# Sixteen-head attentions: parts stored after head 0's copies, head 1's maxima laid beside head 0's scores, units of maxima announced singly

## Chip, cores and metric

One NeuronCore of a Trainium2 chip runs the whole program. The metric is the device time in microseconds (us) of one execution. Three runs of the kernel before took 5205.0, 5204.46 and 5199.28 us; the median is 5204.46 us.

## The reference, cut to what matters

The program is a four-layer hybrid network on 2,048 tokens of width 128. Each step is `x = x + block(layernorm(x))`. Three of its blocks are softmax attentions with 16 heads of width 8, and the change touches these:

```python
# L0_attn_b: rotary, causal.  L2_attn_b and L3_attn_b: every query sees every key.
q, k, v = (x @ Wq + bq), (x @ Wk + bk), (x @ Wv + bv)      # 2048 x 128, 16 heads of 8
s = q_h @ k_h.T / sqrt(8)                                  # per head, 2048 x 2048
p = softmax(s)                                             # L0: keys after the query masked
out = concat_h(p @ v_h) @ Wo + bo
```

A fourth attention (L3_attn_a, local windows) shares the helper that prepares heads, in a variant that is not doubled (below).

## The kernel before, in words

**Splitting and rows.** `prepare_heads` (line 732) splits q and k, each 128 rows (16 heads of 8) by 2,048 tokens in float32, into three bfloat16 parts whose sum is nearly exact (DVE lines 768 to 777, ACT lines 785 to 791), makes two doubled copies of q's lesser parts (line 781) and evicts V (line 794). SP meanwhile copies head 0's 8 rows of each part, SBUF to SBUF, into `qs[0]` and `ks[0]` (`copy_queries`, `copy_keys`, lines 714 to 722: 12 transfers of 32 KB, counted on `rows_in[0]`). ACT then issues the stores of all parts to DRAM (`store_part`, `store_twice`, lines 724 to 729: 8 transfers of 512 KB, counted on `stored`). The block ends when every engine has come to its end, and only then does the next one begin.

**The head loop.** `head_loop` (line 843) is one block in which five engines run their own hand-written orders:

- *Maxima.* PE multiplies 48 rows of bfloat16 parts into scores for a block of 128 queries against up to 1,024 keys (`max_pass`, line 982, matmuls on line 994) and DVE takes the row maximum (line 1133). Such a piece is a unit; there are U = 32 per head without a mask and U = 24 with it. Two PSUM tiles `mps` alternate, so unit x needs unit x - 2 to be taken (line 990). Causal units that cross the diagonal get a mask by another matmul (line 1000). In the causal loop the units of heads 1 and up are issued in pairs, the matmuls of both, then the masks, and one announcement, `mx_ready` plus 2, at the end (line 1001). The first 8 pairs of a head hold an unmasked unit of 1,024 keys and then a masked one of 128 to 512; in the last 4 pairs both are masked.
- *Turn.* After a head's last unit DVE joins its maxima (`join_max`, line 1115), POOL splits them in three (line 427), PE turns them (`turn_max`, line 1003, matmul on line 1008), ACT copies them to `mT` (line 1086), and a DMA puts them into three rows of `qs` (line 1096 on ACT's queue for head 0, line 946 on SP's for the others). DVE joins head h only after unit 0 of head h + 1 (line 1134).
- *Scores.* For each step n of S (S = 64 without a mask, 40 with it) PE computes a tile of 128 keys by up to 512 queries with 123 rows (line 1018), the maximum already subtracted by those three rows, and ACT takes the exponential (line 1105). Three PSUM tiles `sps` alternate. `product` (line 1024) multiplies a group of such tiles by V, 4 or 6 steps late.
- *Copy-out.* After the last product of head h - 1, ACT copies the sums (`copy_out`, line 1088, instruction on line 1092) behind its exponential of step n = OUT = 6 of head h (line 1109). The first product of head h waits for that (line 1028).

**Interleaving.** `due(h, n)` (line 906) says how many units must have been issued by step n of head h. Before the scores begin PE has issued U + 8 units: all of head 0, 3 of head 1, then the turn of head 0, then 5 more of head 1 (lines 1046 to 1053). From then on due rises by U per head, in twos. The turn of head h + 1 stands behind step TURN = S - 7 of head h.

**SP's order.** It waits for all stores (line 957), loads head 1's rows (12 transfers, `load_rows`), then the upper half of head 0's rows (6 transfers on `m_in[0]`), `load_products` of heads 0 and 1 (4 transfers each), a table, then head 2's rows, and from then on one head ahead. `scores` of head h waits on `m_in` (line 1014), `max_pass` of a head's unit 0 on `rows_in` (line 988).

## Time and profile before

| | |
|---|---|
| median of 3 runs | 5204.46 us |
| profiled execution | 5199.7 us (its span in the trace: 5197.9 us) |
| mean granted TensorE clock | 0.918 of 2.4 GHz |
| PE busy | 4488.1 us, 86% of the span, 22,389 matmuls |
| DVE busy | 3223.0 us, 62% |
| ACT busy | 2648.4 us, 51% |
| POOL busy | 976.2 us, 19% |

The causal attention (tiles named 9_heads, 5_head_rows, 8_prepare) lies between 343 and 920 us of the span, the other two (39_heads, 36_head_rows, 38_prepare; and 64_heads, 59_head_rows, 63_prepare) between 2442 and 3185 and between 4164 and 4906 us. In a timeline row stand the start in us, the duration in us of the instructions merged into it, the engine, the line, the operation, output and inputs, the number of instructions, and in brackets how long the engine had been idle and what released it. PEq, ACTq and SPq are the sequencers; a DMA row there is the time in which the transfer was issued, not that in which it moved. A releaser "PEq L755" is the end of the `prepare_heads` block. PEclk is the granted clock: 0.50 is 1.2 GHz, 1.00 is 2.4 GHz.

### The profile page before, as it was taken

The page shows a single profiled execution, that of the slowest core. Times are in us where ns is not written, and L with a number is a line of the kernel's source. Part 1 is how long each engine was busy: PE and PEld are TensorE (multiplying, and loading weights), DVE is VectorE, ACT ScalarE, POOL GpSimd, SP SyncE. Part 2 cuts the span into 40 slices and gives each one's busy share as a digit, 9 for nine tenths or more (in the row PEclk, how much of TensorE's full clock was granted, in tenths as well). Part 3 has the DMA queues.
Part 4 walks back from the last instruction along what each step waited for, and adds up shares of the span by engine and source line. Part 5 has one row for each costly group of instructions (what it writes and reads, how often), then busy time and mean ns, then how long its engine had stood idle before and what let it go on. Part 6 is the DMA issues. An engine that isn't in the chain of part 4 may idle for free. (4 is left out here: it accounts for less than half of the span.)

```text
span 5197.9 us, 65865 instructions
## 1 busy us (share of the span) xinstructions
PE 4488.1 (86%) x22389; PEld 1663.4 (32%) x22441; DVE 3223.0 (62%) x4634; ACT 2648.4 (51%) x4913; POOL 976.2 (19%) x920
## 2 busy tenths in 40 slices
PE   6978888795189999867999997688869889999899
PEld 3432222442033333243122223355544412222244
DVE  4366664435865555254988883437963488888433
ACT  2325666334224444433588885344433348888633
POOL 0000000000038777800000000047940000000000
PEclk8979999897599999978899998898979979999999
DMA  1011110000000000001100000110000010000000
GB/s 62 20 67 35 35 35 20 17 16 0 7 1 3 5 3 5 5 28 37 36 28 28 27 18 2 56 62 3 1 9 16 11 68 26 26 26 26 3 21 20
DMA packets 44620, 118.99 MB, mean 23 GB/s; under 512 B 14463, under 2 KB 15863, under 8 KB 43287
## 3 DMA queue, kind: packets, MB, share of 16 engines
q1 hardware_dynamic: 37235, 98.19, 5.7%
q10 hardware_dynamic: 4524, 15.78, 0.8%
q8 instruction: 166, 2.72, 0.2%
q0 software_dynamic: 2560, 1.19, 0.1%
q14 instruction: 135, 1.11, 0.1%
HBM read 87.89 MB, written 19.01 MB: 21 GB/s over the span
## 5 line engine op out<-in xcount | busy, mean ns | idle before, releaser
L1133 DVE TENSOR_REDUCE 64_heads_mx<-64_heads_mps 128x1 f32<-128x1024 f32 x512 | 604.1, 1220 | 64.3 <-PE 64_heads_mps L994 63.1
L1133 DVE TENSOR_REDUCE 39_heads_mx<-39_heads_mps 128x1 f32<-128x1024 f32 x512 | 604.1, 1220 | 64.3 <-PE 39_heads_mps L994 63.2
L1105 ACT ACTIVATE 64_heads_p<-64_heads_sps 128x512 f32<-128x512 f32 x1024 | 552.8, 596 | 111.2 <-PE 64_heads_sps L1018 107.3
L1105 ACT ACTIVATE 39_heads_p<-39_heads_sps 128x512 f32<-128x512 f32 x1024 | 552.7, 596 | 111.3 <-PE 39_heads_sps L1018 107.3
L2106 ACT ACTIVATE 27_latent_heads_p<-27_latent_heads_ring 128x512 f32<-128x512 f32 x512 | 277.3, 595 | 385.4 <-PE 27_latent_heads_ring L2025 374.1
L1133 DVE TENSOR_REDUCE 9_heads_mx<-9_heads_mps 128x1 f32<-128x1024 f32 (+7 forms) x384 | 334.2, 908 | 179.7 <-PE 9_heads_mps L1000 173.3
L2124 DVE TENSOR_REDUCE 27_latent_heads_mx<-27_latent_heads_ring 128x1 f32<-128x512 f32 x512 | 323.1, 684 | 197.4 <-PE 27_latent_heads_ring L2005 197.4
L1105 ACT ACTIVATE 9_heads_p<-9_heads_sps 128x512 f32<-128x512 f32 (+3 forms) x640 | 304.3, 535 | 190.0 <-PE 9_heads_sps L1021 161.6
L1018 PE MATMUL 64_heads_sps<-59_head_rows_qs,59_head_rows_ks 123*128 123x512 bf16 x1024 | 311.3, 386 | 4.9 <-ACT 64_heads_p L1105 4.9
L1018 PE MATMUL 39_heads_sps<-36_head_rows_qs,36_head_rows_ks 123*128 123x512 bf16 x1024 | 310.9, 385 | 5.2 <-ACT 39_heads_p L1105 5.2
L1981 POOL TENSOR_TENSOR 27_latent_heads_psum<-27_latent_heads_psum,27_latent_heads_p 128x1024 f32<-128x1024 f32 x112 | 263.1, 2349 | 87.8 <-ACT 27_latent_heads_p L2106 87.8
L2021 PE MATMUL 27_latent_heads_ring<-27_latent_heads_qc,23_mla_mem_keys 64*128 64x512 f32 x1024 | 272.7, 609 | 3.4 <-DMA 24_mla_loop_mem_mrow<-27_latent_heads_mT 3.4
L1042 PE MATMUL 39_heads_ops<-39_heads_p,L2b_v 128*9 128x512 f32 x2048 | 267.8, 595 | 0.2 <-ACT 39_heads_osb L1092 0.2
L1042 PE MATMUL 64_heads_ops<-64_heads_p,L3b_v 128*9 128x512 f32 x2048 | 267.8, 595 | 0.2 <-ACT 64_heads_osb L1092 0.2
L1976 POOL TENSOR_TENSOR 27_latent_heads_psum<-27_latent_heads_psum,27_latent_heads_p 128x1024 f32<-128x1024 f32 x112 | 263.3, 2351 | 23.0 <-ACT 27_latent_heads_p L2106 23.0
L2005 PE MATMUL 27_latent_heads_ring<-23_mla_mem_keys,27_latent_heads_qc 64*128 64x512 f32 x1024 | 265.1, 609 | 1.9 <-DVE 27_latent_heads_mx L2124 0.5
L994 PE MATMUL 64_heads_mps<-59_head_rows_ks,59_head_rows_qs 48*128 48x512 bf16 x1024 | 187.6, 403 | 23.3 <-PEq L755 15.3
L994 PE MATMUL 39_heads_mps<-36_head_rows_ks,36_head_rows_qs 48*128 48x512 bf16 x1024 | 187.7, 403 | 18.1 <-PEq L755 10.0
L1018 PE MATMUL 9_heads_sps<-5_head_rows_qs,5_head_rows_ks 123*128 123x512 bf16 (+3 forms) x640 | 183.4, 353 | 11.5 <-ACT 9_heads_p L1105 4.3
L427 POOL CAST 64_heads_mparts<-64_heads_m 128x16 bf16<-128x16 f32 x16 | 3.1, 196 | 973.9 <-DVE 64_heads_m L1119 973.9
L615 DVE TENSOR_TENSOR 4_experts_hg<-4_experts_hr,4_experts_gps 128x512 f32<-128x512 f32 x128 | 88.0, 687 | 147.8 <-ACT 4_experts_hr L602 147.5
L615 DVE TENSOR_TENSOR 67_experts_hg<-67_experts_hr,67_experts_gps 128x512 f32<-128x512 f32 x128 | 88.0, 688 | 146.4 <-ACT 67_experts_hr L602 146.1
(1119 smaller groups left out, 7456.7 us busy)
## 6 DMA issues: line engine op xcount, KB each, us to landing
44_hale_masks_qs<-scratch_q_parts SPq DMA_DIRECT2D x45, 96.0 KB
44_hale_masks_ks<-scratch_k_parts SPq DMA_DIRECT2D x45, 96.0 KB
4_experts_wbuf<-in_L0f_experts SPq DMA_DIRECT2D x8, 514.0 KB, 3.5
12_experts_wbuf<-in_L0f_experts SPq DMA_DIRECT2D x8, 514.0 KB, 3.4
58_experts_wbuf<-in_L3f_experts SPq DMA_DIRECT2D x8, 514.0 KB, 3.5
67_experts_wbuf<-in_L3f_experts SPq DMA_DIRECT2D x8, 514.0 KB, 3.5
5_head_rows_qs<-scratch_q_parts SPq DMA_DIRECT2D x47, 64.0 KB
5_head_rows_ks<-scratch_k_parts SPq DMA_DIRECT2D x47, 64.0 KB
```

What stands on the lines that cost most here:

```text
L615: dve.tensor_tensor(hg[n % SLOTS][:], hr[n % SLOTS][:], gps[n // NF % 2][:], ALU.mult).then_inc(hg_ready, 1)
L994: ins = pe.matmul(mps[x % 2][:, b:b + n], qs[h % SETS][low:low + SIX, tile(i)], ks[h % SETS][low:low + SIX, 1024 * half + b:1024 * half + ...
L1018: ins = pe.matmul(sps[e % SB][:, 0:CW - off], ks[h % SETS][0:SUM_ROWS, tile(j)], qs[h % SETS][0:SUM_ROWS, c * CW + off:(c + 1) * CW], star ...
L1042: ins = pe.matmul(ops[row:row + ROW, off:CW], Vt[:, j, h, :], p, start=(s == 0), stop=(causal or s == NG - 1), tile_position=(0, row), ski ...
L1105: act.activation(pslot[x % PS][:, 0:CW - off], sps[e % SB][:, 0:CW - off], ACT.Exp, scale=SCALE / 2).then_inc(ex_done, 1)
L1133: dve.tensor_reduce(mx[h % 2][:, i, half:half + 1], mps[x % 2][:, 0:w], AX.X, ALU.max).then_inc(mx_taken, 1)
L1976: pool.tensor_tensor(psum[:, 0, :], so_far, slot(p, h)[:], ALU.add).then_inc(added_even, 1)
L1981: pool.tensor_tensor(psum[:, 1, :], so_far, slot(p, h)[:], ALU.add).then_inc(added_odd, 1)
L2005: pe.matmul(bank(number, x)[:], qc[h % 2][half, tile(i)], keys[half, chunk(2 * (u % 2) + x)], start=True, stop=True).then_inc(mx_ready, 1)
L2021: pe.matmul(bank(number, x)[:], keys[half, tile(j)], qc[h % 2][half, chunk(2 * (p % 2) + x)], start=True, stop=False)
L2106: act.activation(slot(p, h)[:, x * CW:(x + 1) * CW], bank(score_number(p, h), x)[:], ACT.Exp, scale=MLA_SCALE).then_inc(ex_done, 1)
L2124: dve.tensor_reduce(mx[:, w // NC, w % NC:w % NC + 1], bank(max_number(w // 2, h), w % 2)[:], AX.X, ALU.max).then_inc(mx_taken, 1)
```

## The change

1. `store_part` and `store_twice` become one `store`. With `doubled` (the three 16-head attentions) ACT no longer calls it in `prepare_heads` but at the start of `head_loop`, after a wait for `rows_in[0]` to reach 12 transfers. Without `doubled` ACT issues the same stores at the same place, behind all its waits instead of part by part.
2. New constants FIRST and WAIT: (0, 8) causal, (4, 0) otherwise. Before the scores PE issues U + FIRST units in place of U + 8, with the turn of head 0 after U + FIRST / 2. In head 0 `due` rises from U + FIRST along a steeper line, from step WAIT on, until it meets the old one; for heads 1 and up it is as before.
3. OUT is 4 instead of 6 in the causal loop.
4. SP loads head 1's rows behind head 0's upper rows and products.
5. Each unit announces itself: an unmasked one behind its own matmuls, a masked one behind its mask.
6. DVE joins head 0's maxima ahead of unit 0 of head 1; for later heads the join stays behind unit 0.

```diff
@@ -721,12 +721,12 @@
             if a == b:
                 eng.dma_start(self.ks[0][DH * i:DH * (i + 1), :], self.k[a][0:DH, :]).then_inc(self.rows_in[0], 16)
 
-    def store_part(self, g, eng, a):
-        eng.dma_start(g.scratch["q_parts"][a], self.q[a][:]).then_inc(self.stored, 16)
-        eng.dma_start(g.scratch["k_parts"][a], self.k[a][:]).then_inc(self.stored, 16)
-
-    def store_twice(self, g, eng, n):
-        eng.dma_start(g.scratch["q_parts"][3 + n], self.twice[n][:]).then_inc(self.stored, 16)
+    def store(self, g, eng):
+        for a in range(3):
+            eng.dma_start(g.scratch["q_parts"][a], self.q[a][:]).then_inc(self.stored, 16)
+            eng.dma_start(g.scratch["k_parts"][a], self.k[a][:]).then_inc(self.stored, 16)
+        for a, t in enumerate(self.twice):
+            eng.dma_start(g.scratch["q_parts"][3 + a], t[:]).then_inc(self.stored, 16)
 
 
 def prepare_heads(g, qT, kT, Vt, Wv, bv, weights, rows):
@@ -793,13 +793,11 @@
                 for c in range(NC):
                     act.activation(Vt[:, c * TPC:(c + 1) * TPC, :, 0:DH], vps[c][:].rearrange("p (t h d) -> p t h d", t=TPC, d=DH),
                                    ACT.Identity).then_inc(v_done, 1)
-                for a in range(3):
+                if not doubled:
                     for s in "qk":
-                        wait_for_part(act, s, a)
-                    rows.store_part(g, act, a)
-                for n in range(len(twice)):
-                    act.wait_ge(two_done, n + 1)
-                    rows.store_twice(g, act, n)
+                        for a in range(3):
+                            wait_for_part(act, s, a)
+                    rows.store(g, act)
 
             @block.sync
             def _(sp):
@@ -853,10 +851,11 @@
     U = len(units)
     SB, PS = 3, 12
     AHEAD = 8
+    FIRST, WAIT = (0, 8) if causal else (4, 0)
     TURN = S - 7
     LATE = 4 if causal else 6
     BURST = 2
-    OUT = 6
+    OUT = 4 if causal else 6
     A = P // HEADS
     N = HEADS * S
     qs, ks, rows_in = rows.qs, rows.ks, rows.rows_in
@@ -903,13 +902,19 @@
         def turned(h):
             return 0 if h == 0 else 2 + (h - 1) * (S + 1) + TURN
 
+
+
         def due(h, n):
-            return min(HEADS * U, U + AHEAD + h * U + (n + 1) * U // (S * BURST) * BURST)
+            steady = min(HEADS * U, U + AHEAD + h * U + (n + 1) * U // (S * BURST) * BURST)
+            if h:
+                return steady
+            begun = max(0, n + 1 - WAIT)
+            return min(steady, U + FIRST + begun * (U - FIRST) // ((TURN - 5 - WAIT) * BURST) * BURST)
 
         def group_of(n):
             return next(j for j, gr in enumerate(groups) if gr[0][0] <= n <= gr[-1][0])
 
-        assert U + AHEAD + (TURN - 4) * U // S >= 2 * U
+        assert due(0, TURN) >= 2 * U
 
         with nc.Block() as block:
             @block.gpsimd
@@ -955,11 +960,11 @@
 
                 sp.wait_ge(rows.filled, rows.FILLED)
                 sp.wait_ge(rows.stored, rows.STORED)
-                load_rows(sp, 1)
                 for a in range(3):
                     load_queries(g, sp, 0, a, qs[0], m_in[0], (1,))
                     load_keys(g, sp, 0, a, ks[0], m_in[0], (1,))
                 load_products(sp, 0)
+                load_rows(sp, 1)
                 load_products(sp, 1)
                 sp.dma_start(spread[:], g.big["head_spread"].rearrange("p (a q) -> p a q", q=P)).then_inc(spread_in, 16)
                 for h in range(HEADS):
@@ -994,11 +999,12 @@
                             ins = pe.matmul(mps[x % 2][:, b:b + n], qs[h % SETS][low:low + SIX, tile(i)],
                                             ks[h % SETS][low:low + SIX, 1024 * half + b:1024 * half + b + n],
                                             start=True, stop=not (diag and b + n == w))
+                        if not diag:
+                            ins.then_inc(mx_ready, 1)
                     for x in xs:
                         _i, _half, w, diag = units[x % U]
                         if diag:
-                            ins = pe.matmul(mps[x % 2][:, w - P:w], g.ident_bf[:], g.mask_q[:], start=False, stop=True)
-                    ins.then_inc(mx_ready, len(xs))
+                            pe.matmul(mps[x % 2][:, w - P:w], g.ident_bf[:], g.mask_q[:], start=False, stop=True).then_inc(mx_ready, 1)
 
                 def turn_max(h):
                     e = turned(h)
@@ -1044,11 +1050,11 @@
                     ins.then_inc(pv_done, 1)
 
                 x = 0
-                while x < U + 3:
+                while x < U + FIRST // 2:
                     max_pass([x])
                     x += 1
                 turn_max(0)
-                while x < U + AHEAD:
+                while x < U + FIRST:
                     max_pass([x])
                     x += 1
                 late = []
@@ -1091,6 +1097,9 @@
                         act.wait_ge(o_out[h % 2], STORED * (h // 2))
                     act.activation(osb[h % 2][:], ops[:], ACT.Identity).then_inc(o_copied, 1)
 
+
+                act.wait_ge(rows_in[0], SIX_COPIED)
+                rows.store(g, act)
                 copy_max(0)
                 act.wait_ge(ex_done, 1)
                 act.dma_start(qs[0][TWICE:SUM_ROWS, :], mT[0][:]).then_inc(m_in[0], 16)
@@ -1129,9 +1138,11 @@
                     i, half, w, _d = units[u]
                     if u == 0 and h >= 2:
                         dve.wait_ge(m_joined, h - 1)
+                    if u == 0 and h == 1:
+                        join_max(0)
                     dve.wait_ge(mx_ready, x + 1)
                     dve.tensor_reduce(mx[h % 2][:, i, half:half + 1], mps[x % 2][:, 0:w], AX.X, ALU.max).then_inc(mx_taken, 1)
-                    if u == 0 and h:
+                    if u == 0 and h >= 2:
                         join_max(h - 1)
                 join_max(HEADS - 1)
                 for i in range(2):
```

## Rows read from the trace of the kernel before

**Rows 1.** Windows, causal and first unmasked attention: length, busy (count) by engine, PEclk, DMA.
```profile
343.00:920.00 577.00, 487.99 (x3128) 140.16 (x3128) 347.86 (x420) 328.06 (x687) 20.66 (x88) 0.94 0.12 40
2442.00:3185.00 743.00, 711.56 (x4152) 147.90 (x4152) 616.92 (x545) 575.02 (x1071) 16.39 (x80) 0.96 0.09 30
```

**Rows 2.** Waits of PE, 440 to 881 us: who for whom, total us, times, longest.
```profile
PE 9_heads_mps L994 <- DVE 9_heads_mx L1133: 23.4, 41, 0.8
PE 9_heads_ops L1039 <- ACT 9_heads_osb L1092: 11.8, 14, 0.8
PE 9_heads_sps L1008 <- POOL 9_heads_mparts L431: 6.2, 13, 0.5
```

**Rows 3.** Timeline of one copy-out of the causal loop.
```profile
568.95 1.47 ACT L1105 ACTIVATE 9_heads_p<-9_heads_sps 128x384 f32<-128x384 f32 x3 [0.97 <-PE 9_heads_sps L1021]
569.83 0.38 PE L1018 MATMUL 9_heads_sps<-5_head_rows_qs,5_head_rows_ks 123*128 123x512 bf16 x1
570.29 0.62 ACT L1092 ACTIVATE 9_heads_osb<-9_heads_ops 128x512 f32<-128x512 f32 x1
571.06 1.06 PE L1039 MATMUL 9_heads_ops<-9_heads_p,9_heads_Vz 128*25 128x512 f32 x8 [0.84 <-ACT 9_heads_osb L1092]
```

**Rows 4.** Timeline around the turn of head 1, causal loop.
```profile
426.79 0.39 PE L994 MATMUL 9_heads_mps<-5_head_rows_ks,5_head_rows_qs 48*128 48x512 bf16 x2
...
427.82 1.23 DVE L1133 TENSOR_REDUCE 9_heads_mx<-9_heads_mps 128x1 f32<-128x1024 f32 x1 [0.55 <-PE 9_heads_mps L1000]
...
430.63 0.24 PE L1008 MATMUL 9_heads_sps<-ident_bf,9_heads_mparts 128*48 128x128 bf16 x1 [0.48 <-POOL 9_heads_mparts L431]
...
432.59 0.49 PE L994 MATMUL 9_heads_mps<-5_head_rows_ks,5_head_rows_qs 48*128 48x512 bf16 x3
...
433.28 1.56 DVE L1133 TENSOR_REDUCE 9_heads_mx<-9_heads_mps 128x1 f32<-128x1024 f32 x2 [1.67 <-PE 9_heads_mps L1000]
...
434.57 0.61 PE L994 MATMUL 9_heads_mps<-5_head_rows_ks,5_head_rows_qs 48*128 48x512 bf16 x3 [0.77 <-DVE 9_heads_mx L1133]
```

**Rows 5.** Timeline, one pair of units of the unmasked loop in its steady part.
```profile
2515.15 0.60 PE L994 MATMUL 39_heads_mps<-36_head_rows_ks,36_head_rows_qs 48*128 48x512 bf16 x4
2515.58 2.36 DVE L1133 TENSOR_REDUCE 39_heads_mx<-39_heads_mps 128x1 f32<-128x1024 f32 x2 [0.50 <-PE 39_heads_mps L994]
```

**Rows 6.** Timeline, from the preparation into the causal head loop.
```profile
356.19 0.36 ACTq L725 DMA_DIRECT2D scratch_q_parts<-5_head_rows_q  x1
...
357.49 0.62 ACT L794 ACTIVATE L0b_v<-8_prepare_vps 128x512 f32<-128x512 f32 x1
...
361.46 2.39 ACTq L729 DMA_DIRECT2D scratch_q_parts<-5_head_rows_twice  x2
...
364.32 1.12 PE L994 MATMUL 9_heads_mps<-5_head_rows_ks,5_head_rows_qs 48*128 48x512 bf16 x3 [8.31 <-PEq L755]
...
367.81 1.92 SPq L818 DMA_DIRECT2D 5_head_rows_qs<-scratch_q_parts  x2
```

**Rows 7.** Timeline, first unmasked attention: into the loop, head 0's turn, first scores.
```profile
2455.26 0.61 ACT L794 ACTIVATE L2b_v<-38_prepare_vps 128x512 f32<-128x512 f32 x1
...
2461.51 1.86 PE L994 MATMUL 39_heads_mps<-36_head_rows_ks,36_head_rows_qs 48*128 48x512 bf16 x4 [9.97 <-PEq L755]
...
2502.90 0.30 PE L1008 MATMUL 39_heads_sps<-ident_bf,39_heads_mparts 128*48 128x128 bf16 x1 [0.85 <-POOL 39_heads_mparts L431]
...
2507.87 1.90 PE L1018 MATMUL 39_heads_sps<-36_head_rows_qs,36_head_rows_ks 123*128 123x512 bf16 x4
```

**Rows 8.** Timeline, causal attention: head 0's turn and first scores.
```profile
396.38 0.30 PE L1008 MATMUL 9_heads_sps<-ident_bf,9_heads_mparts 128*48 128x128 bf16 x1 [0.86 <-POOL 9_heads_mparts L431]
...
404.07 0.61 PE L1018 MATMUL 9_heads_sps<-5_head_rows_qs,5_head_rows_ks 123*128 123x512 bf16 x1 [4.04 <-DMA 5_head_rows_qs<-9_heads_mT]
```

**Rows 9.** Windows: unmasked head 0's maxima, and causal head 0's first scores.
```profile
2462.00:2502.00 40.00, 34.09 (x70) 4.38 (x68) 39.63 (x38) 0.00 (x0) 0.38 (x2) 0.50 0.28 98
404.00:410.00 6.00, 5.83 (x22) 1.58 (x26) 2.21 (x3) 3.88 (x8) 0.00 (x0) 0.62 0.08 31
```

## Prediction

> **What bounds the kernel now.** I read the windows of the attentions first. In the causal one PE is busy 488.0 of 577 us, in the first unmasked one 711.6 of 743 us [rows 1]. So the unmasked loop is full of PE work, and what its steady part could give is small; the causal one leaves 89 us in which PE stands. I then asked PE's waits in the causal loop's steady part: over 441 us, 23.4 us go to DVE's maxima, 11.8 us to the copy-out and 6.2 us to the split ahead of a turn [rows 2]. These come once or a few times per head; over the 13 to 14 heads of that stretch the 41.4 us are 3.0 us a head. Last I read the starts of the three loops, which each come once.
>
> **Part 1, copy-out at step 4 instead of 6 (causal).** ACT's exponentials of steps 4, 5 and 6 begin at 568.95 and take 1.47 us together, the copy-out begins at 570.29, and PE, free at 569.83 + 0.38 = 570.21, waits until 571.06: 0.84 us [rows 3]. Behind step 4 alone (a third of 1.47, 0.49) the copy-out begins at about 569.4 and ends at 570.0, before PE arrives. The last product of the head before was issued at step 3, so it is there. The exponentials of steps 5 and 6 come 0.62 us later; the next score needs that of step 5, done at 570.5, and comes only behind the 1.06 us of products, so this is covered. PE is the bound, so 0.84 us are saved in each of 15 heads: -12.6 us (from below 0, if ACT hands the delay on, to -12.6).
>
> **Part 2, one announcement per unit (causal).** An unmasked unit is ready 0.43 us after its first matmul starts [rows 5]. Around the turn the pair starts at 426.79, so DVE could start at 427.22 and starts at 427.82; it is free by 427.3, so the reduce, the join and the split come 0.5 us earlier, and PE's wait of 0.48 us at the turn goes [rows 4]. That is 14 turns (2 to 15) by 0.48: -6.7 us. At the second pair after the turn PE waits 0.77 us for the reduce that began at 433.28, 0.69 us behind its matmuls at 432.59; with 0.43 in place of 0.69 the wait shrinks by 0.26 [rows 4]. The waits among doubly masked pairs lose only what lies between two masks, some 0.06. So 0.32 by 14.5 heads: -4.6 us. PE's instructions stay the same in number. Bounds: 0 to -12; I take -11.3. In the unmasked loops each unit announced itself already, and OUT stays: 0.
>
> **Part 3, the stores leave the preparation (all three).** ACT finished its last eviction at 358.11, but went on issuing stores until 363.85, and PE started at 364.32 [rows 6]: 0.47 us from ACT's end to PE's start. Now ACT's end is 358.11 and PE starts at about 358.5, if head 0's copies are there; SP issued the last of them before ACT's evictions began, and without stores beside them I expect them just in time: -5.8 us. In the unmasked attention ACT ends at 2455.87 (no row of V's product delays it there), so ACT's end alone would give 2456.3 for 2461.51 [rows 7]; no row shows when the copies landed, which were issued about 1 us later against ACT's end, and I take 2457.0: -4.5 us each (bounds -5.2 to -3). Bounds in the causal one: -6 to -5. What the stores now delay: issuing began at 356.19 and now begins at about 358.6, so SP's first load moves by the same 2.4 us, from 367.81 to some 370.2 [rows 6]. Head 0's ten transfers come first now and have 25 us until they are needed; head 1's twelve come some 10 us behind them, at about 390, while head 0's maxima end at about 388. With WAIT = 8 they are wanted only from 400 on: 0. ACT has nothing else to do in that time.
>
> **Part 4, the join ahead of head 1's unit 0.** It saves one reduce of 1.2 us less its overlap, [rows 4] has 1.23: -1.1 us in each attention.
>
> **Part 5, from head 0's turn to its first score.** In the causal attention it was 404.07 - 396.38 = 7.69 us, and what ended it was the 12 KB transfer of the turned maxima: PE had been idle for 4.04 us when it landed [rows 8]. SP's loads were under way beside it. They still are: 0. In the unmasked one it was 4.97 us, and PE was filling it with units, not waiting [rows 7]. Now only 2 units stand there, about 2.3 us, and the transfer is issued some 5.6 us earlier while SP's loads end 2 to 3 us later, so it lies in the middle of them as the causal one did: 7.7 us, +2.7 each. Bounds: 4.2 (the shortest that the 4.97 us allow) to 10 if a longer queue delays it. I take the causal row because the traffic beside it is the nearer case.
> The Trainium skill (DMA: Bandwidth & Descriptors, Queues, rings and completion order) says that each DMA engine goes round between the queues it has work for, a packet at a time. By that rule the transfer does not wait for the whole queue of loads; the trace agrees in part, since 31 GB/s were still moving in the 6 us after it had landed [rows 9], but not in that the way from the turn to its landing took 7.7 us.
>
> **Part 6, head 0's scores carry more maxima.** Causal: 8 units that lay under the 7.7 us of part 5 come into steps 9 to 29. PE's share is 4 pairs by 0.6: +2.4 us, the lower bound. But DVE now has 24 units, the join and the split between step 9 and the turn. DVE works 347.9 / 16 = 21.7 us per head [rows 1]; with unit 0 of head 2 (1.2), join and split (1.6), and gaps of about 0.7 in each of four doubly masked pairs (2.8) that is 27.3 us, and step 9 is reached some 6.5 us after the first score. From first score to turn: 33.8 us against 430.63 - 404.07 = 26.6 us [rows 4, 8]. +7 us (2.4 to 8.5). This is what the change pays. Unmasked: 4 units by 0.30 [rows 5], +1.2, and the pair with unit 0 of head 2 falls on step 55 rather than 51 while the turn stays at 57, so 2.6 us of slack go and PE waits about 2.0 us there: +3.2 each (1.2 to 4.5).
>
> **Sum.** Causal: -12.6 - 11.3 - 5.8 - 1.1 + 0 + 7 = -23.8. Unmasked, twice: -4.5 - 1.1 + 2.7 + 3.2 = +0.3, so +0.6. Together -23.2 us against the profiled 5199.7 us, which gives 5176.5 us. The median of the runs shown is 4.8 us above the profiled execution, so the same against the median is 5181 us; I say 5180.
>
> **Rivals.** (a) *The maxima's transfer lands quickly*, in 4.2 us after the turn instead of 7.7, because it shares its engines with the loads packet by packet. Then part 5 is -3.5 in the causal and -0.8 rather than +2.7 in each unmasked attention: 10.5 us better, 5170. For it: the unmasked transfer landed within 4.97 us. Against it: 7.69 us in the causal attention [rows 8]. The rule of the Trainium skill (DMA: Bandwidth & Descriptors, same section) is on this side. (b) *The copy-out's wait comes back on ACT*: two exponentials come 0.62 us later, and if PE then meets them at its three score tiles, part 1 gives nothing: 5180 + 12.6 = 5193, a bare change. Against it is that the score behind the copy-out has 0.6 us to spare. (c) *Slower*: the clock. In the 40 us of unmasked maxima PE was busy 34.1 us and still got 0.50; in causal head 0 it was busy 5.8 of the first 6 us and got on average 0.62, rising to full [rows 9]. If head 0's scores, which DVE now paces and holds up, leave PE at 1.2 GHz until head 0 ends, its work of 488.0 / 16 = 30 us in the causal and 711.6 / 16 = 44 us in each unmasked head [rows 1] takes twice that. Less the waits already counted (7 and 3 us) this is +23 and twice +41 us: 5181 + 105 = 5286 us. It decides if the granted clock is still 0.50 ten us into head 0's scores; against it stands that before it rose within those ten. (d) *Announcing singly starts nothing earlier*, the reduces begin behind the mask as now: 5191.
>
> **How the numbers follow.** The sum 0.60, (a) 0.20, (b) 0.11, (c) 0.04, (d) 0.05. Gathering the ends of the bounds on the good side (transfer quick, PE's share alone in part 6) gives about -40, on the bad side, without (c), about -10: 5163 to 5193, which leaves out (c) and little else. About 0.2% (10.4 us) is what a measurement of this kernel can tell from no change. (b) lies near that bound and goes half to no change; with the worst of the sum that is 0.09 no change, 0.04 slower, 0.87 faster.
>
> **What would show it.** Right: no PE wait for 9_heads_osb; PE's wait for the split gone in heads 2 to 15; the causal loop's turns 1.6 us closer together than before; the first max matmul about 0.4 us behind the last eviction; 33 to 35 us from the causal loop's first score to its second turn; some 2 us of PE wait at the second turn of each unmasked loop. Wrong: turns less than 0.8 us closer, a first max matmul later than 360, or a granted clock of 0.50 ten us into head 0's scores.

## The result: 0.18% faster, less than half of the forecast

| | before | after |
|---|---|---|
| median of 17 runs each | 5204.72 us | 5194.85 us |
| profiled execution (its span) | 5199.7 us (5197.9) | 5189.27 us (5187.5) |
| mean granted TensorE clock | 0.918 | 0.917 |

The ratio is 0.9982, with a 95% interval of 0.9975 to 0.9989: 9.9 us faster where about 24 were forecast. The interval leaves out 1, so it is a gain, but it lies just inside the 0.2% that the prediction took as its bound for "no change", and outside the predicted 5163 to 5193 us.

Whole-kernel shares don't show where the gain went: PE is busy 4494.0 us in the changed kernel, 5.9 more than before, and the other engines differ by less than 2.

So I cut each attention at events that every kernel here has: the first cast of the preparation, the first max matmul, head 0's turn, the first score, and the turns of heads 1, 2, ... up to 15. Each number is the difference of two start times in the timeline. C is the causal attention, U1 and U2 the unmasked ones.

| us | C before | C after | U1 before | U1 after | U2 before | U2 after |
|---|---|---|---|---|---|---|
| preparation to first max matmul | 20.8 | 14.7 | 19.1 | 13.9 | 19.1 | 13.9 |
| turn 0 to first score | 7.7 | 7.7 | 5.0 | 7.8 | 5.0 | 7.7 |
| turn 0 to turn 1 | 34.25 | 44.31 | 42.22 | 50.55 | 42.22 | 50.54 |
| turn 1 to turn 2 | 32.30 | 30.56 | 42.10 | 45.99 | 42.09 | 47.32 |
| each later pair of turns (median) | 32.29 | 30.50 | 42.09 | 42.08 | 42.09 | 42.08 |
| **preparation to turn 15** | **537.6** | **515.8** | **691.6** | **697.5** | **691.7** | **698.9** |

The last line gives -21.8, +5.9 and +7.2, together -8.6 of the 10.4 us between the two spans. The prediction had -23.8 and twice +0.3: the causal attention came to nearly the sum forecast for it, and each unmasked one paid 5.6 or 6.9 us that the prediction didn't see.

**The steady causal loop** is as forecast. PE's waits from 440 to 850 us, in the form of [rows 2], have lost the copy-out and the split. DVE's maxima are left, and waits of up to 0.3 us for an exponential:

```profile
PE 9_heads_mps L999 <- DVE 9_heads_mx L1144: 19.2, 41, 0.7
PE 9_heads_sps L1024 <- ACT 9_heads_p L1114: 3.3, 13, 0.3
```

The waits for exponentials aren't new. The kernel before has them too, from 440 to 881 us, in a row that [rows 2] doesn't show:

```profile
PE 9_heads_sps L1018 <- ACT 9_heads_p L1105: 3.3, 13, 0.3
```

The timeline around one copy-out and one turn of the changed kernel answers to [rows 3, 4]. The copy-out (L1098) starts behind one exponential instead of three, 0.5 us ahead of the score, the products (L1045) follow without a wait, and so does the turn (L1014). At the second pair of maxima after it PE waits 0.51 instead of 0.77 us:

```profile
552.14 0.23 PE L1014 MATMUL 9_heads_sps<-ident_bf,9_heads_mparts 128*48 128x128 bf16 x1
...
555.84 0.61 PE L999 MATMUL 9_heads_mps<-5_head_rows_ks,5_head_rows_qs 48*128 48x512 bf16 x3 [0.51 <-DVE 9_heads_mx L1144]
...
561.05 0.49 ACT L1114 ACTIVATE 9_heads_p<-9_heads_sps 128x384 f32<-128x384 f32 x1 [0.97 <-PE 9_heads_sps L1027]
561.44 0.59 ACT L1098 ACTIVATE 9_heads_osb<-9_heads_ops 128x512 f32<-128x512 f32 x1
561.93 0.38 PE L1024 MATMUL 9_heads_sps<-5_head_rows_qs,5_head_rows_ks 123*128 123x512 bf16 x1
562.24 1.06 PE L1045 MATMUL 9_heads_ops<-9_heads_p,9_heads_Vz 128*25 128x512 f32 x8
```

**The three starts**, from the timeline of the changed kernel, beside [rows 6, 7, 8]. The first max matmul of the causal attention starts at 354.80, 0.31 us behind ACT's last eviction, which ended at 354.49. In the first unmasked one, PE waited for head 0's copies in the end, so these were not quite there:

```profile
352.43 2.06 ACT L794 ACTIVATE L0b_v<-8_prepare_vps 128x512 f32<-128x512 f32 x4 [0.87 <-PE 8_prepare_vps L763]
...
354.80 0.65 PE L999 MATMUL 9_heads_mps<-5_head_rows_ks,5_head_rows_qs 48*128 48x512 bf16 x3 [2.41 <-PEq L755]
...
385.78 0.30 PE L1014 MATMUL 9_heads_sps<-ident_bf,9_heads_mparts 128*48 128x128 bf16 x1 [2.78 <-POOL 9_heads_mparts L431]
...
393.48 0.61 PE L1024 MATMUL 9_heads_sps<-5_head_rows_qs,5_head_rows_ks 123*128 123x512 bf16 x1 [7.40 <-DMA 5_head_rows_qs<-9_heads_mT]
...
2432.10 1.82 PE L999 MATMUL 39_heads_mps<-36_head_rows_ks,36_head_rows_qs 48*128 48x512 bf16 x4 [4.82 <-DMA 36_head_rows_ks<-36_head_rows_k]
...
2472.44 0.30 PE L1014 MATMUL 39_heads_sps<-ident_bf,39_heads_mparts 128*48 128x128 bf16 x1 [0.99 <-POOL 39_heads_mparts L431]
...
2480.19 1.91 PE L1024 MATMUL 39_heads_sps<-36_head_rows_qs,36_head_rows_ks 123*128 123x512 bf16 x4 [6.26 <-DMA 36_head_rows_qs<-39_heads_mT]
```

**Where the unmasked attentions lost.** Here is the timeline of head 0's scores and the start of head 1's, in the changed kernel:

```profile
2496.99 0.39 PE L999 MATMUL 39_heads_mps<-36_head_rows_ks,36_head_rows_qs 48*128 48x512 bf16 x2 [0.32 <-DVE 39_heads_mx L1144]
2498.12 0.39 PE L999 MATMUL 39_heads_mps<-36_head_rows_ks,36_head_rows_qs 48*128 48x512 bf16 x2 [0.74 <-DVE 39_heads_mx L1144]
...
2522.99 0.24 PE L1014 MATMUL 39_heads_sps<-ident_bf,39_heads_mparts 128*48 128x128 bf16 x1 [2.17 <-POOL 39_heads_mparts L431]
...
2524.14 0.84 PE L1024 MATMUL 39_heads_sps<-36_head_rows_qs,36_head_rows_ks 123*128 123x512 bf16 x2
...
2526.84 1.49 PE L1048 MATMUL 39_heads_ops<-39_heads_p,L2b_v 128*9 128x512 f32 x8
...
2530.51 0.39 PE L999 MATMUL 39_heads_mps<-36_head_rows_ks,36_head_rows_qs 48*128 48x512 bf16 x2 [0.79 <-DVE 39_heads_mx L1144]
2531.64 0.39 PE L999 MATMUL 39_heads_mps<-36_head_rows_ks,36_head_rows_qs 48*128 48x512 bf16 x2 [0.74 <-DVE 39_heads_mx L1144]
```

The 2.17 us at turn 1 are the predicted 2.0. What follows them was not predicted: two scores take 0.84 us (0.61 at full clock, as at 2528.26), eight products 1.49 (1.05). Then two pairs of maxima, at 2528.80 and 2530.51, come close together and PE waits twice more for DVE. The windows, in the columns of [rows 1] with GB/s at the end, show the granted clock behind the turn in U1 and in U2, where it fell twice:

```profile
2522.00:2527.00 5.00, 4.01 (x21) 0.73 (x25) 2.07 (x3) 1.83 (x4) 0.73 (x4) 0.74 0.01 2
2527.00:2532.00 5.00, 3.47 (x20) 0.56 (x12) 3.69 (x4) 2.28 (x5) 0.00 (x0) 0.92 0.06 12
...
4251.00:4256.00 5.00, 4.03 (x17) 0.60 (x17) 1.18 (x2) 1.40 (x4) 0.71 (x4) 0.66 0.01 2
4256.00:4261.00 5.00, 3.51 (x21) 0.81 (x20) 4.76 (x5) 2.73 (x5) 0.00 (x0) 1.00 0.07 22
4261.00:4266.00 5.00, 5.00 (x25) 0.63 (x24) 3.74 (x4) 2.77 (x5) 0.00 (x0) 0.66 0.25 89
```

And these windows run from turn 1 to turn 2, in U1 of the kernel before and then in U1 and U2 of the changed one. PE is busy for 2.4 and 3.7 us more, and has 262 matmuls for 258:

```profile
2545.12:2587.22 42.10, 42.07 (x258) 8.62 (x257) 37.80 (x34) 35.18 (x67) 1.02 (x5) 1.00 0.08 26
...
2522.99:2568.98 45.99, 44.44 (x262) 8.89 (x262) 38.51 (x34) 34.45 (x65) 1.02 (x5) 0.96 0.07 24
4251.97:4299.29 47.32, 45.81 (x262) 8.87 (x262) 38.52 (x34) 34.46 (x65) 1.02 (x5) 0.93 0.07 23
```

The four matmuls are a pair of units, and the diff says where it comes from. In the unmasked loops the new `due` doesn't meet the old one within head 0: at its last step, 63, it asks for 70 units where the old one asks for 72. From head 1 on the old one holds and asks for 72 at step 0. So a pair that used to come before turn 1 comes behind it, one step behind the pair of step 63.

### The profile page after: what moved, and what is told of

Read it like the earlier page. It is cut to its first block and busy times, and to the rows that moved or that the text cites. A ratio compares the mean times of both kernels' runs of the same rounds, so it can differ in the third digit from the quotient of the medians.

```text
span 5187.5 us, 65847 instructions
## 1 busy us (share of the span) xinstructions
PE 4494.0 (87%) x22389; PEld 1664.0 (32%) x22441; DVE 3221.5 (62%) x4634; ACT 2646.9 (51%) x4913; POOL 976.2 (19%) x920
## 5 line engine op out<-in xcount | busy, mean ns | idle before, releaser
L999 PE MATMUL 64_heads_mps<-59_head_rows_ks,59_head_rows_qs 48*128 48x512 bf16 x1024 | 187.4, 403 | 18.6 <-DMA 59_head_rows_ks<-59_head_rows_k 10.1
L1024 PE MATMUL 9_heads_sps<-5_head_rows_qs,5_head_rows_ks 123*128 123x512 bf16 (+3 forms) x640 | 185.2, 355 | 14.7 <-DMA 5_head_rows_qs<-9_heads_mT 7.4
L615 DVE TENSOR_TENSOR 58_experts_hg<-58_experts_hr,58_experts_gps 128x512 f32<-128x512 f32 x128 | 88.0, 687 | 146.1 <-ACT 58_experts_hr L602 145.8
```

What stands on the lines that cost most here:

```text
L615: dve.tensor_tensor(hg[n % SLOTS][:], hr[n % SLOTS][:], gps[n // NF % 2][:], ALU.mult).then_inc(hg_ready, 1)
L999: ins = pe.matmul(mps[x % 2][:, b:b + n], qs[h % SETS][low:low + SIX, tile(i)], ks[h % SETS][low:low + SIX, 1024 * half + b:1024 * half + ...
L1024: ins = pe.matmul(sps[e % SB][:, 0:CW - off], ks[h % SETS][0:SUM_ROWS, tile(j)], qs[h % SETS][0:SUM_ROWS, c * CW + off:(c + 1) * CW], star ...
```

## The theory, and its rivals

Theory: the copy-out and the announcements give their 24.6 us in the causal attention (turn 1 to turn 15, 425.8 us for 450.4); the early stores and the join give theirs at all three starts; and the new pace of head 0 takes most of that back, by DVE's waits, by the wait at turn 1 and by the clock after it. The first rival is that the early stores themselves cost it, because they push SP's loads into the transfer of the maxima. The second is that the shorter cover ahead of the first score does.

### 1. The copy-out and the announcements alone

From the kernel before:

```diff
-    OUT = 6
+    OUT = 4 if causal else 6
...
+                        if not diag:
+                            ins.then_inc(mx_ready, 1)
...
-                            ins = pe.matmul(mps[x % 2][:, w - P:w], g.ident_bf[:], g.mask_q[:], start=False, stop=True)
-                    ins.then_inc(mx_ready, len(xs))
+                            pe.matmul(mps[x % 2][:, w - P:w], g.ident_bf[:], g.mask_q[:], start=False, stop=True).then_inc(mx_ready, 1)
```

> The kernel before with two parts alone: one announcement per causal unit, and OUT = 4 in the causal loop. Pacing theory (the missing gain is lost in heads 0 and 1 of each attention, because maxima moved beside head 0's scores let DVE pace PE, and a fall of the granted clock follows): these two parts lose nothing there, so the causal turns come 30.50 us apart as in the changed kernel (32.29 before), the unmasked ones stay at 42.1 us, and the whole is 25 to 27 us faster than before, 5178. Traffic rival (the loss is in late loads): the same here. If a part of the 1.79 us per head came from elsewhere in the change (the join, the loads' order), the turns lie between 30.5 and 32.3 us.

Measured: 5178.64 us (4 runs; before on that chip 5202.08), ratio 0.9955 (0.9938 to 0.9972). The causal attention took 515.6 us from preparation to turn 15, its turns lie 30.50 us apart, and both unmasked ones took the old 691.6. PE's waits from 440 to 850 us have one row besides those for exponentials, as in the changed kernel:

```profile
PE 9_heads_mps L994 <- DVE 9_heads_mx L1134: 19.2, 41, 0.7
```

So these two parts alone end where the whole change ends in the causal attention, at 515.6 against 515.8 us, and lose nothing in the other two. The equality is partly luck. From turn 1 to turn 15 both take 425.8 us, but this run spent 2.6 us more ahead of turn 1 than the kernel before, where its edit leaves the order of PE's work as it was: 1.3 us to the first max matmul (22.2 for 20.8) and 1.3 from turn 0 to turn 1 (35.55 for 34.25), where the granted clock was still 0.50 over the 9.4 us behind the first score. Against the kernel before, the change gains 7.2 us up to turn 0 of C and loses 10.1 from there to turn 1: 2.8 us lost on balance. The whole is 23.4 us faster where 25 to 27 were expected.

### 2. The stores alone

From the kernel before, the eight stores go from `prepare_heads` to the start of ACT's part of the head loop; SP's order, the join and the pace stay:

```diff
-                for a in range(3):
+                for a in range(0 if doubled else 3):
...
-                for n in range(len(twice)):
-                    act.wait_ge(two_done, n + 1)
-                    rows.store_twice(g, act, n)
...
+                act.wait_ge(rows_in[0], SIX_COPIED)
+                for a in range(3):
+                    rows.store_part(g, act, a)
+                for n in range(len(rows.twice)):
+                    rows.store_twice(g, act, n)
                 copy_max(0)
```

> The kernel before with the stores moved behind head 0's copies and nothing else. Both theories: the first max matmul comes 6.1 us (causal) and 5.2 us (unmasked) earlier against the preparation. Pacing theory: from turn 0 to turn 1 34.3 us in the causal attention and 42.2 to 45 us in the unmasked ones (the transfer of the turned maxima may take 7.7 us instead of under 5), from turn 1 to turn 2 42.1 us; in all 11 to 16 us faster than before. Traffic rival: the later loads fall beside heads 0 and 1, so turn 1 to turn 2 takes 46 to 47 us in the unmasked attentions as in the changed kernel and the whole gains 2 to 5 us.

Measured: 5194.19 us, one run. The first max matmul comes 15.4 us after the preparation's start in C (20.8 before), 13.9 in U1 and in U2. Of this 5.1 to 5.5 us, C keeps 4.7 to turn 15 (532.9), U1 and U2 3.0 and 2.9 (688.6, 688.8): from turn 0 to the first score they now take 7.2 and 7.4 us instead of 5.0. C took 35.51 us from turn 0 to turn 1, as in experiment 1. So the stores give more than they cost, and the first rival holds for some 2.3 us in each unmasked attention and no more. The other sign of it, 46 to 47 us from turn 1 to turn 2, is absent (42.09 and 42.08). The stages gain 10.6 us where 11 to 16 were expected, the single run 5.5 against the profiled execution of before: between the attentions, in code that no kernel here changes, it took 5.2 us longer.

### 3. The changed kernel with the old pace in the unmasked loops

```diff
-    FIRST, WAIT = (0, 8) if causal else (4, 0)
+    FIRST, WAIT = (0, 8) if causal else (8, 0)
...
-            if h:
+            if h or not causal:
...
-                while x < U + FIRST // 2:
+                while x < U + (0 if causal else 3):
```

> The changed kernel, but in the two unmasked attentions the number of units ahead of the scores (8), the place of head 0's turn (behind 3 of them) and due are as before. Pacing theory: there turn 0 to turn 1 takes 42 to 45 us instead of 50.5 and turn 1 to turn 2 takes 42.1 instead of 46.0 and 47.3; the causal attention is as in the changed kernel; in all 17 to 25 us faster than the changed kernel, 5170 to 5177. Traffic rival: turn 1 to turn 2 stays at 46 to 47 us and the gain against the changed kernel is at most 10 us.

Measured: 5181.27 us (4 runs), ratio 0.9953 (0.9936 to 0.9969), 13.6 us below the changed kernel's median. U1 took 689.0, U2 688.3 us to turn 15, with 42.09 and 42.08 from turn 1 to turn 2. Between U2's first score and turn 1 PE doesn't wait at all. These are PE's waits from 4209 to 4252 us in the changed kernel:

```profile
PE 64_heads_sps L1024 <- DMA 59_head_rows_qs<-64_heads_mT: 6.2, 1, 6.2
PE 64_heads_sps L1014 <- POOL 64_heads_mparts L431: 2.2, 1, 2.2
PE 64_heads_mps L999 <- DVE 64_heads_mx L1144: 1.2, 3, 0.7
PE 64_heads_sps L1024 <- ACT 64_heads_p L1114: 0.8, 3, 0.3
```

and this is all of them from 4212 to 4250 us in the experiment:

```profile
PE 64_heads_sps L1024 <- DMA 59_head_rows_qs<-64_heads_mT: 1.9, 1, 1.9
```

So the pace is what the unmasked attentions lost by: 8.5 and 10.6 us. The stages are together 19.0 us below the changed kernel's, inside the 17 to 25 that were expected; the median is only 13.6 below, and the profiled execution, at 5182.59 us, only 6.7. In that one, the stretch between U1 and U2, whose code is the same, took 8.5 us longer (see the last section).

### 4. The changed kernel with head 2's row loads held back

```diff
                         if h:
                             sp.wait_ge(sc_ready, entry(h - 1, S - 1) + 1)
+                        else:
+                            sp.wait_ge(sc_ready, entry(0, 0) + 1)
                         load_rows(sp, h + 2)
```

> The changed kernel, with SP holding head 2's rows and products back until head 0's first score is out. If the transfer of the turned maxima is slow because head 2's loads share its engines, the time from turn 0 to the first score falls from 7.7 us to 3.5 to 5 us in the unmasked attentions, less in the causal one, where head 1's loads are still under way; 6 to 9 us faster than the changed kernel. If the 7.7 us are the transfer's own, it stays at 7.7 us and nothing is gained. Traffic rival for the rest: the loads held back come later, so heads 0 and 1 lose more, turn 1 to turn 2 over 47 us; pacing theory: that stays at 46 to 47 us.

Measured: 5184.74 us, one run. In U1 and U2 the first score comes 2.9 us after the turn instead of 7.7 (3.5 to 5 expected), in C still 7.6. The timeline of U1:

```profile
2475.40 0.30 PE L1016 MATMUL 39_heads_sps<-ident_bf,39_heads_mparts 128*48 128x128 bf16 x1 [0.99 <-POOL 39_heads_mparts L431]
...
2478.30 1.91 PE L1026 MATMUL 39_heads_sps<-36_head_rows_qs,36_head_rows_ks 123*128 123x512 bf16 x4 [1.41 <-DMA 36_head_rows_qs<-39_heads_mT]
```

In these 2.9 us the DMA engines moved 4 GB/s, and 55 in the changed kernel from 2473.0 to 2480.2. So in these loops the transfer of the turned maxima is slow only beside SP's loads; in C it is head 1's loads that lie there, which this edit doesn't hold. The shorter cover, the second rival, is worth nothing once the transfer is quick. Yet U1 and U2 still take 691.3 and 693.6 us: the wait of 2.17 us at turn 1 and the long stretch from turn 1 to turn 2 (44.47 and 46.07) are still there. The pace costs by itself. But the clock need not follow: behind the same wait in U1 it stayed at 1.00, and only in U2 did it fall.

```profile
2521.12:2565.59 44.47, 42.96 (x262) 8.90 (x262) 38.55 (x34) 34.45 (x65) 1.02 (x5) 1.00 0.08 25
```


### 5. The copy-out alone

From the kernel before, only `OUT = 4 if causal else 6`.

> The kernel before with OUT = 4 in the causal loop and nothing else. The prediction's term: the copy-out's wait of 0.84 us per head goes, so the causal turns come 31.45 us apart (32.29 before), in all 12 to 13 us faster than before. Rival (the wait comes back on ACT): turns 31.8 to 32.3 us apart. The rest of the measured 1.79 us per head, 0.95 us, is then the announcements' (predicted 0.80).

Measured: 5188.07 us, one run (before on that chip 5204.69). Turns 31.38 us apart: 0.91 us a head, predicted 0.84. PE's waits from 440 to 875 us beside [rows 2]:

```profile
PE 9_heads_mps L994 <- DVE 9_heads_mx L1133: 23.4, 41, 0.8
PE 9_heads_sps L1008 <- POOL 9_heads_mparts L431: 6.3, 13, 0.5
PE 9_heads_ops L1039 <- ACT 9_heads_osb L1092: 0.2, 1, 0.2
```

The copy-out's 11.8 us are gone and the other two rows untouched, so the remaining 0.88 us a head of experiment 1 (31.38 to 30.50) are the announcements', predicted 0.80.

### 6. The changed kernel with a steeper pace in the unmasked head 0

```diff
-            return min(steady, U + FIRST + begun * (U - FIRST) // ((TURN - 5 - WAIT) * BURST) * BURST)
+            return min(steady, U + FIRST + begun * (U - FIRST) // ((TURN - (5 if causal else 9) - WAIT) * BURST) * BURST)
```

It puts the pair with unit 0 of head 2 back at step 51, and packs the rest of head 0 tighter.

> The changed kernel with a steeper due in head 0 of the unmasked attentions (it meets the old line at step 47, so the pair that holds unit 0 of head 2 comes at step 51 as before; 4 units ahead of the scores as in the changed kernel). If the loss behind turn 1 hangs on PE's wait at that turn and on the pairs that pile up behind it, turn 1 shows no wait, turn 1 to turn 2 takes 42.1 to 43 us and the clock stays at 1.00 there, while turn 0 to turn 1 stays at 49 to 51 us since DVE has as many units to take: 8 to 11 us faster than the changed kernel. If it is DVE's pace in head 0 that lets the clock fall, the fall comes in head 0 and turn 0 to turn 1 grows over 51 us; if it is the traffic, turn 1 to turn 2 stays at 46 to 47 us.

Measured: 5187.97 us, one run. No wait at turn 1, and turn 1 to turn 2 is back at 42.08 and 42.09 us. But turn 0 to turn 1 stays at 50.39 and rises to 51.75, and PE's waits in U2 from 4211 to 4256 us show what replaced it:

```profile
PE 64_heads_sps L1024 <- DMA 59_head_rows_qs<-64_heads_mT: 6.1, 1, 6.1
PE 64_heads_mps L999 <- DVE 64_heads_mx L1144: 2.6, 6, 0.7
PE 64_heads_sps L1024 <- ACT 64_heads_p L1114: 0.5, 2, 0.3
```

That is 2.6 us for 1.2: DVE has as many units to take, so the wait at the turn is spread over three more. U2 is 1.2 us longer than in the changed kernel although PE waits less there; from 4211 to 4216 and from 4216 to 4221 us the granted clock was 0.50 and 0.64, while the changed kernel had 1.00 from 4214 to 4219. Behind turn 1, the granted clock is full in this kernel, in the columns of [rows 1]:

```profile
4250.00:4255.00 5.00, 5.00 (x32) 1.00 (x32) 4.59 (x6) 4.11 (x9) 1.03 (x5) 1.00 0.01 2
```

So the 3.9 and 5.2 us from turn 1 to turn 2 go when three things go together, which this run doesn't part: the wait at turn 1, the late pair (this `due` asks for 72 units at step 63, as the old one does), and the two close pairs behind the turn.

### 7. The changed kernel with the old pace everywhere

`due` returns the old line, FIRST = AHEAD, and three units of head 1 stand before turn 0 again:

```diff
-                while x < U + FIRST // 2:
+                while x < U + 3:
```

> The changed kernel with the old pace in all three attentions (head 0's turn behind 3 units of head 1, 8 ahead of the scores, the old due). Unmasked: as with the old pace there alone, from the preparation to turn 15 688 to 689 us. Causal: if the pace alone costs, turn 0 to turn 1 takes 34 to 36 us instead of 44.3, and from the preparation to turn 15 about 507 to 511 us instead of 516; if head 1's rows land too late for units ahead of the turn (SP now loads them last), turn 0 is 2 to 5 us later than in the changed kernel and the gain is eaten, 511 to 516. In all 5 to 9 us faster than with the old pace in the unmasked attentions alone, 5172 to 5177.

Measured: 5174.79 us (4 runs), ratio 0.9944 (0.9929 to 0.996). C took 512.1 us. Head 1's first units now wait for head 1's rows ahead of the turn:

```profile
393.72 0.71 PE L996 MATMUL 9_heads_mps<-5_head_rows_ks,5_head_rows_qs 48*128 48x512 bf16 x3 [7.19 <-DMA 5_head_rows_ks<-scratch_k_parts]
...
396.19 0.30 PE L1011 MATMUL 9_heads_sps<-ident_bf,9_heads_mparts 128*48 128x128 bf16 x1
...
404.31 0.61 PE L1021 MATMUL 9_heads_sps<-5_head_rows_qs,5_head_rows_ks 123*128 123x512 bf16 x1 [3.75 <-DMA 5_head_rows_qs<-9_heads_mT]
```

Turn 0 comes 52.7 us after the preparation's start (45.7 in the changed kernel), and still the attention is 3.8 us shorter, since turn 0 to turn 1 takes 33.56 instead of 44.31 us.

### 8. Old pace, the turn first, head 2's loads held back

```diff
-    FIRST, WAIT = (0, 8) if causal else (4, 0)
+    FIRST = AHEAD
...
-            if h:
-                return steady
-            begun = max(0, n + 1 - WAIT)
-            return min(steady, U + FIRST + begun * (U - FIRST) // ((TURN - 5 - WAIT) * BURST) * BURST)
+            return steady
...
+                        else:
+                            sp.wait_ge(sc_ready, entry(0, 0) + 1)
...
-                while x < U + FIRST // 2:
+                while x < U + (0 if causal else 2):
```

> The old due everywhere, but head 0's turn right behind its own units (causal) or behind 2 of head 1's (unmasked), 8 units ahead of the scores, and head 2's loads held back until the first score. Pace theory: the units of head 1 run under the transfer of the turned maxima, which takes 3 us in the unmasked attentions (as with the loads held back) and up to 7.7 us in the causal one; turn 0 to first score 6 to 7 us in the unmasked ones (6 units by 1.13 us), turn 0 to turn 1 43.5 to 44.5 us, turn 1 to turn 2 42.1 us; causal turn 0 to turn 1 36 to 38 us. In all the fastest of these kernels, 5168 to 5174. If held back loads then come too late for heads 1 and 2, turn 1 to turn 2 grows over 43 us.

Measured: 5163.24 us (5 runs, 5160.22 to 5168.88; before 5204.69), ratio 0.9923 (0.991 to 0.9937). It beats both kernels, and the 5168 to 5174 us that were expected. C took 508.1 us, U1 686.4, U2 686.8; against before that is -29.5, -5.2 and -4.9, together -39.6, and the profiled executions differ by 39.5. In C the turn goes first, the units of head 1 wait 4.13 us for their rows behind it, and the transfer of the maxima lands meanwhile:

```profile
387.86 0.30 PE L1013 MATMUL 9_heads_sps<-ident_bf,9_heads_mparts 128*48 128x128 bf16 x1 [2.79 <-POOL 9_heads_mparts L431]
...
392.29 0.71 PE L998 MATMUL 9_heads_mps<-5_head_rows_ks,5_head_rows_qs 48*128 48x512 bf16 x3 [4.13 <-DMA 5_head_rows_ks<-scratch_k_parts]
...
398.92 0.63 PE L1023 MATMUL 9_heads_sps<-5_head_rows_qs,5_head_rows_ks 123*128 123x512 bf16 x1
```

## Why the prediction was wrong, step by step

**Parts 1 and 2** were right: 0.91 and 0.88 us a head for 0.84 and 0.80 (experiments 5 and 1). Rival (b), the wait coming back on ACT, and rival (d), announcements that start nothing, fell with them. PE's waits for exponentials are 3.3 us, 13 times, before and after, so nothing came back on ACT.

**Part 3** was right in size: the first max matmul is 6.1 us closer to the preparation's start in C, 5.2 in U1 and in U2, for 5.8 and 4.5. Taking the copies as just in time was close: in U1 PE waited for them, at 2432.10.

**Part 4** was right. From the preparation's start to turn 0 C went from 52.9 to 45.7 us, 7.2 for the 6.9 of parts 3 and 4 together, and U1 from 60.4 to 54.2, 6.2 for 5.6.

**Part 5** was right: 7.7 us from turn to first score in all three, for 7.7. Rival (a), a quick transfer, was wrong for this kernel. Experiment 4 shows why it is slow: with the loads held back it took 2.9 us in the unmasked loops, which is also less than the 4.2 that the prediction gave as the shortest. The Trainium skill (DMA: Bandwidth & Descriptors, Queues, rings and completion order) says that an engine serves its queues in turn, packet by packet; the transfer did land while loads were still to come, as the rule has it (in C 64 GB/s were moving in the 6.5 us behind its landing), but 7.7 against 2.9 us from the turn to the first score is what lying beside the loads costs a 12 KB transfer here.

**Part 6 is the step that failed**, in the causal attention by size and in the unmasked ones by mechanism: it put what happens behind turn 1 at nothing, and it took DVE to keep up wherever the average rates fit.

- Causal: turn 0 to turn 1 went up by 10.1 us, not 7; less the unchanged 7.7 us this is 26.6 to 36.6 us of scores for a predicted 33.8. DVE's pace was the right cause. PE's waits from 391 to 431 us in the changed kernel are

```profile
PE 9_heads_mps L999 <- DVE 9_heads_mx L1144: 6.1, 11, 0.8
```

  and those from 404 to 431 us in the kernel before, the same work without head 1's first units:

```profile
PE 9_heads_mps L994 <- DVE 9_heads_mx L1133: 1.0, 2, 0.7
```

  That is 5.1 us, less the 0.5 at the turn that is gone, and PE's added share 2.4. The remaining 3.0 of 10.1 us fit the granted clock, which these windows of the changed kernel show falling in the midst of the waits; in the kernel before it was 1.00 from 421 to 431 us. From the first score to turn 1 its mean was 0.85 for 0.92. No run took the clock by itself.

```profile
416.00:421.00 5.00, 3.31 (x26) 0.95 (x18) 3.71 (x5) 1.81 (x5) 0.00 (x0) 1.00 0.00 0
421.00:426.00 5.00, 3.89 (x19) 0.82 (x20) 3.39 (x4) 0.36 (x2) 0.00 (x0) 0.58 0.01 3
426.00:431.00 5.00, 5.00 (x31) 1.46 (x34) 2.53 (x4) 2.90 (x7) 1.02 (x5) 0.74 0.00 0
```

- Unmasked: first score to turn 1 took 42.8 instead of 37.25 us, +5.5 for +3.2. The wait at turn 1 was right (2.17 for 2.0), but PE's share was not placed right: of the four units two come ahead of turn 1 and the late pair behind it. What the step left out is that `due` is a staircase: two units every three or four steps. The pair at 2496.99 comes three steps, 1.7 us, behind the one before, DVE's 2.36 us for a pair [rows 5] are not done, and PE waits (1.2 us in three waits in U2) although on average DVE keeps up. With 0.8 us of waits for exponentials PE waits 4.2 us in all in U2, and is busy 1.3 us more. Experiment 6 shows that a steeper slope doesn't mend it.
- Unmasked, turn 1 to turn 2: +3.9 and +5.2 us for a predicted 0. This was missed altogether, and it has three parts. Head 0's last pair and the late pair at head 1's step 0 stand close together and add waits of 0.79 + 0.74 = 1.5 us. The late pair itself is 0.6 us of PE. And behind the wait at turn 1 the granted clock fell; PE, being the bound there, ran part of its next work at 1.2 GHz. By subtraction 1.8 and 3.1 us are the clock's, whose mean from turn 1 to turn 2 was 0.96 and 0.93 for 1.00. The first two parts are sure: in U1 of experiment 4 they are there without any fall, and the stretch takes 2.4 us too long. That the wait is what makes the clock fall is argued: the fall came behind three of four such waits, and experiment 6, without the wait, has neither fall nor excess.

Rival (c) had named the clock, but as one event that lasts through head 0 and costs 105 us. It came as short falls in each attention, some 2 to 3 us each. Giving it a chance of its own in that extreme form kept it out of the sum, where it belonged with a small price.

Together the unmasked attentions came out at +5.9 and +7.2 for +0.3 each, 12.5 us, and the causal one at 21.8 for 23.8, 2.0 us. That is the whole gap of the stages, 23.2 to 8.6.

The assumption beneath part 6 was also never weighed: that head 0's work before its scores must be cut at all. In C, three units of head 1 lay under head 0's join and split and five under the transfer, and both had to be waited for anyway; they cost nothing there. Moved among the scores they cost 10 us. In C the rows of head 1 are late for those units (experiment 7: landed 50.2 us after the preparation's start), which the change answers with WAIT = 8; experiment 8 instead lets PE wait 4.13 us for the rows behind the turn, beside the transfer, and is 7.7 us shorter in that attention.

## What to carry to other kernels

Work that stands under a wait which will come anyway is free; before moving it into a stretch paced by another engine, compare that engine's time for one burst with the shortest distance between two bursts, not the averages. Where a new schedule hands over to the old one, count what each has asked for by then: here a pair was left over and landed beside another. Price a new wait of the bounding engine at its length plus what the clock may take after it: here the same 2.17 us were followed by nothing once, by 1.8 us twice and by 3.1 us once. And when a change bundles several parts, measure the parts that act in every head without those that act once: here they alone gave more than all of it.

## What the runs showed of the hardware

- Behind a wait of 2.17 us on PE, after a stretch in which it had other short waits, the granted clock fell from 1.00 (2.4 GHz) to a mean of 0.74 over the 5 us from about the turn in the changed kernel's U1 and 0.66 in U2. In U2 it was 1.00 over the 5 us after that, and 0.66 over the next 5. In experiment 4 it stayed at 1.00 behind the same wait in U1.
- Waits of at most 0.8 us, eleven between 391 and 431 us, came with a fall in the changed kernel's C: 0.58 from 421 to 426 us.
- The clock's rise at the start of head 0's scores varies with the same order of work: its mean over the 10 us behind C's first score was 0.53 in experiment 1, and in the kernel before it was 0.62 over the first six and 1.00 from 409 us.
- With a 12 KB transfer between two SBUF tiles on the way, it is 2.9 us from turn to first score while the DMA engines move 4 GB/s, and 7.7 beside loads that make it 55.
- Stretches with the same code differ between kernels by up to 10 us, as much as the whole change gave. Between U1's turn 15 and U2's preparation the profiled executions took 1030.6 us (before), 1031.4 (after), 1029.9 (experiment 8), but 1039.9 in experiment 3 and 1039.0 in experiment 7. The window from 320 to 400 us behind U1's turn 15 shows a granted clock of 0.86 and 0.87 in the changed kernel and experiment 8, and 0.77 in experiment 7; these are the changed kernel's and experiment 7's rows:

```profile
3435.70:3515.70 80.00, 61.02 (x789) 39.47 (x777) 30.86 (x47) 33.01 (x55) 23.69 (x60) 0.86 0.11 33
```

```profile
3424.80:3504.80 80.00, 64.90 (x782) 40.97 (x782) 25.51 (x31) 29.80 (x47) 24.15 (x59) 0.77 0.11 36
```

  What sets it off there is open: there is one profiled execution of each. That is why the readings above rest on the stages, with the medians beside them.
